# A decoder layer on one Trainium2 core: the key bias added on VectorE, rows normalised on ScalarE

## What is computed

```python
x = x + attention(layernorm(x))        # then cross-attention, then experts
q = xn @ Wq + bq;  k = xn @ Wk + bk;  v = xn @ Wv + bv
Q = elu(q) + 1;    K = elu(k) + 1
KV = einsum('nshd,nshv->nhdv', K, v / L)
Z = 1 / (einsum('nlhd,nhd->nlh', Q, K.sum(axis=1)) + 1e-6)
out = einsum('nlhd,nhdv,nlh->nlhv', Q, KV, Z) * L
```

## Time and profile before

| | |
|---|---|
| median of 3 runs | 1554.05 us (1553.39 to 1558.0) |
| the profiled execution | 1552.01 us, its span 1550.3 us |
| busy over the span: PE, DVE, ACT, POOL | 93%, 40%, 37%, 24% |
| the chain that ended last, by engine | PE 81%, DMA 5%, DVE 4%, issue 4%, POOL 3%, ACT 2% |
| the front | 0 to 293 us |
| TensorE's granted clock, mean | 0.97 of full speed |

### The profile page before, as it was taken

How to read it: one execution, slowest core, us unless ns; L and a number is a source line. 1 busy time by engine, 2 the same in 40 slices (tenths; PEclk the granted TensorE clock), 3 DMA queues, 4 the chain that set the end, 5 groups by cost and what they waited for, 6 DMA issues and landing times.

```text
span 1550.3 us, 20985 instructions
## 1 busy us (share of the span) xinstructions
PE 1447.4 (93%) x7326; PEld 1214.5 (78%) x7327; DVE 623.7 (40%) x1383; ACT 568.7 (37%) x977; POOL 366.3 (24%) x354
## 2 busy tenths in 40 slices
PE   5999999999984499999999899999999999999998
PEld 4867887788772387888888788898789888897886
DVE  5634565467875243411342431215441431215211
ACT  4433433257865233312342531224431422214211
POOL 3201232137665302011112112021112112021011
PEclk9999999999996699999999999999999999999999
DMA  9100221219445426211253432026532342035112
GB/s 198 54 1 28 82 82 55 82 73 219 130 117 173 130 90 163 61 34 20 67 172 54 126 91 41 2 52 184 148 88 54 107 109 41 0 54 149 14 41 27
DMA packets 80537, 132.20 MB, mean 85 GB/s; under 512 B 31940, under 2 KB 32068, under 8 KB 79464
## 3 DMA queue, kind: packets, MB, share of 16 engines
q1 hardware_dynamic: 63816, 97.41, 21.4%
q0 software_dynamic: 16672, 34.16, 11.8%
HBM read 93.64 MB, written 37.91 MB: 85 GB/s over the span
## 4 chain that ended last, share of the span: by engine, by line
PE 81%; DMA 5%; DVE 4%; issue 4%; POOL 3%; ACT 2%; SPq 0%; ACTq 0%; DVEq 0%; POOLq 0%
PE pg L947 16%; PE pg L948 16%; PE pg L949 15%; PE pj L947 8%; PE pj L949 8%; PE pj L948 8%; DMA stage<-w 2%; DMA slot_table<-pack,dest 2%; POOL slot_table L601 2%; PE pt L1301 1%; PE pg L1144 1%; PE pj L1178 1%; DVE w_lo L1364 1%; PE pt L965 1%; DMA out_rows<-ost,etab 1%
## 5 line engine op out<-in xcount | busy, mean ns | idle before, releaser
L947 PE MATMUL pg<-xe_hi,w_hi 128*128 128x512 f32 (+2 forms) x1088 | 393.9, 362 | 22.3 <-DVE w_lo L1364 12.4
L948 PE MATMUL pg<-xe_lo,w_hi 128*128 128x512 f32 (+2 forms) x1088 | 393.0, 361 | 0.0
L949 PE MATMUL pg<-xe_hi,w_lo 128*128 128x512 f32 (+2 forms) x1088 | 392.4, 361 | 0.0
L1755 DVE TENSOR_TENSOR hp<-gl,pg 128x512 f32<-128x512 f32 (+1 forms) x136 | 87.1, 641 | 606.2 <-ACT gl L900 606.2
L678 POOL DMA_INDIRECT out_rows<-ost,etab x62 | 99.8, 1610 | 781.5 <-issue 405.6
L947 PEld LDWEIGHTS pg<-xe_hi,w_hi 128*128 128x128 f32 x1088 | 207.5, 191 | 54.1 <-DVE w_lo L1364 14.4
L900 ACT ACTIVATE gl<-pg 128x512 f32<-128x512 f32 (+1 forms) x136 | 76.1, 560 | 457.2 <-PE pg L949 457.1
L949 PEld LDWEIGHTS pg<-xe_hi,w_lo 128*128 128x128 f32 x1088 | 207.6, 191 | 28.4
L948 PEld LDWEIGHTS pg<-xe_lo,w_hi 128*128 128x128 f32 x1088 | 207.5, 191 | 28.4
L947 PE MATMUL pj<-w_hi,hg_hi 128*128 128x512 f32 x464 | 183.3, 395 | 0.0
L949 PE MATMUL pj<-w_hi,hg_lo 128*128 128x512 f32 x464 | 180.7, 390 | 0.0
(11 more groups left out here) (238 smaller groups left out, 1951.3 us busy)
## 6 DMA issues: line engine op xcount, KB each, us to landing
stage<-w SPq DMA_DIRECT2D x96, 512.0 KB, 4.9
xr<-x SPq DMA_DIRECT2D x8, 1024.0 KB, 8.6
out_rows<-xr SPq DMA_DIRECT2D x8, 1024.0 KB, 7.3
x_rows<-xn SPq DMA_DIRECT2D x8, 1024.0 KB, 6.4
x_in<-x SPq DMA_DIRECT2D x7, 1024.0 KB, 5.2
late_xT<-xT_hi SPq DMA_DIRECT2D x2, 1024.0 KB, 3.9
late_xT<-xT_lo SPq DMA_DIRECT2D x2, 1024.0 KB, 5.9
xT_hi<-late_xT SPq DMA_DIRECT2D x2, 1024.0 KB, 4.7
```

What stands on the lines that cost most here:

```text
L947: nc.tensor.matmul(o, lh, rh, start=start, stop=False)
L948: nc.tensor.matmul(o, lh, rl, start=False, stop=False)
L949: return nc.tensor.matmul(o, ll, rh, start=False, stop=stop)
L1755: v.tensor_tensor(hp[j % 2][:, 0:w], gl[j % 2][:, 0:w], pg[:, 2 + j % 2, 0:w], ALU.mult).then_inc(s_hp, 1)
```

## The change

VectorE has a new step `key_bias`: it adds `bk_all` (the bias on all partitions, loaded by one broadcast transfer) to a key job's bank and writes `kb[j % 2]` in SBUF. ScalarE's exp and relu of key jobs read `kb`. TensorE's 32 bias products go, with `ones_r`, `bk_parts` and their preparation on ScalarE and VectorE, and TensorE's wait for a key bank is now for `s_kb` (VectorE has added) and no longer for `s_feat`. ScalarE's first `wk_hi` waits for `wk_raw` alone.

In each step j of VectorE's loop `key_bias(s, j)` is the first thing, and its feature job is that of j - 1, the `k_lo` that of j - 2. `xn_lo` is made by tiles (`rows_lo`), and the next group's statistics are split in two and two; tiles, statistics and `aggregate` lie between the jobs of steps 0 and 1, the first two statistics ahead of them. Group 0 keeps its four statistics together at the end of step 2.

The rows are normalised on ScalarE (`normalise`, scale and bias from `rstd` and `shift`), behind `k_hi` 1 in step 2, in group 0 behind job 4 and `k_hi` 3 in step 4; VectorE does group 0's own. GpSimd makes `shift` with two more small operations (`neg_mean`, and its product with `rstd`) ahead of the signal.

```diff
...
@@ -192,9 +191,8 @@
     wv_sb = fr("wv_sb", [P, KC, D])
-    ones_r = fr("ones_r", [P, P], F32R)
-    bk_parts = fr("bk_parts", [P, D], F32R)
-    bk_rows = fr("bk_rows", [BR, D])
+    bk_all = fr("bk_all", [P, D])
+    kb = [fr(f"kb{i}", [P, D]) for i in range(2)]
     bv_row = fr("bv_row", [1, D])
...
@@ -372,7 +371,7 @@
         table_t = table[0:TRASH, :].rearrange("(t p) w -> p t w", p=P)
-        XATTN_LOADS, WOUT_LOADS, WK_LOADS, WQ_LOADS, WV_LOADS = 7, 5, 3, 2, 2
+        XATTN_LOADS, WOUT_LOADS, WK_LOADS, WQ_LOADS, WV_LOADS = 7, 5, 1, 2, 2
 
@@ -389,9 +388,8 @@
                 sp.dma_start(x_in[:, i, :], x_g[0][:, i, :]).then_inc(s_x0[i], 16)
-            for dst, src in ((wk_raw[:], wk.rearrange("(k p) n -> p k n", p=P)),
-                             (bk_rows[0:1, :], bk), (bk_rows[BR - 1:BR, :], bk)):
-                sp.dma_start(dst, src).then_inc(s_wk_in, 16)
+            sp.dma_start(wk_raw[:], wk.rearrange("(k p) n -> p k n", p=P)).then_inc(s_wk_in, 16)
+            sp.dma_start(bk_all[:], bk.broadcast_to([P, D])).then_inc(s_bk, 16)
             for dst, src in ((wq_raw[:], wq.rearrange("(k p) n -> p k n", p=P)), (bq_c[:], bq)):
@@ -423,7 +421,7 @@
             sp.wait_ge(s_xnhi, GROUPS)
-            sp.wait_ge(s_xnlo, GROUPS)
+            sp.wait_ge(s_xnlo, GROUPS * TI)
             sp.dma_start(xr[1][:], x_g[1]).then_inc(s_xr[1], 16)
@@ -515,7 +513,13 @@
                 pool.wait_ge(s_stat, s + 1)
-                inverse_std(0).then_inc(s_rstd, 1)
+                if s == 0:
+                    inverse_std(0).then_inc(s_rstd, 1)
+                    return
+                pool.wait_ge(s_xn, s)
+                p.tensor_scalar(neg_mean[0][:], mv[0][:, :, 0], -1.0, None, ALU.mult)
+                step(inverse_std(0))
+                p.tensor_tensor(shift[0][:], neg_mean[0][:], rstd[0][:], ALU.mult).then_inc(s_rstd, 1)
 
@@ -701,13 +705,8 @@
 
-            a.activation(ones_r[:], ones[:], ACT.Copy).then_inc(s_yev, 1)
-            a.activation(bk_parts[:], zrow[:], ACT.Copy).then_inc(s_bk, 1)
             act.wait_ge(s_wk_in, 16 * WK_LOADS)
             a.activation(wk_hi[:], wk_raw[:], ACT.Copy).then_inc(s_whi, 1)
-            act.wait_ge(s_bk, 1)
-            a.activation(bk_parts[0:1, :], bk_rows[0:1, :], ACT.Copy)
-            a.activation(bk_parts[BR - 1:BR, :], bk_rows[BR - 1:BR, :], ACT.Copy).then_inc(s_whi, 1)
 
@@ -718,12 +717,27 @@
             def job(s, j):
-                act.wait_ge(s_proj, FIRST[s] + j + 1)
+                if j < TI:
+                    act.wait_ge(s_kb, s * TI + j + 1)
+                else:
+                    act.wait_ge(s_proj, FIRST[s] + j + 1)
                 if s or j >= 2:
                     act.wait_ge(s_fm, FIRST[s] + j - 1)
-                bias = 0.0 if j < TI else bq_c[:, j - TI:j - TI + 1]
-                a.activation(fe[j % 2][:], pj[j % 2][:], ACT.Exp, bias=bias)
-                a.activation(frl[j % 2][:], pj[j % 2][:], ACT.Relu, bias=bias).then_inc(s_feat, 1)
+                from_, bias = (kb[j % 2], 0.0) if j < TI else (pj[j % 2], bq_c[:, j - TI:j - TI + 1])
+                ins = a.activation(fe[j % 2][:], from_[:], ACT.Exp, bias=bias)
+                if s == 0 and j == 0:
+                    ins.then_inc(s_yev, 1)
+                a.activation(frl[j % 2][:], from_[:], ACT.Relu, bias=bias).then_inc(s_feat, 1)
+
+            def normalise(s):
+
+                act.wait_ge(s_rstd, s + 1)
+                act.wait_ge(s_xnhi, s)
+                act.wait_ge(s_xnlo, s * TI)
+                for i in range(TI):
+                    ins = a.activation(xn[:, i, :], x_in[:, i, :], ACT.Identity, bias=shift[0][:, i:i + 1],
+                                       scale=rstd[0][:, i:i + 1])
+                ins.then_inc(s_xn, 1)
 
@@ -757,6 +771,8 @@
                         khi(s, j - 1)
+                    if s + 1 < GROUPS and j == (TI if s == 0 else 2):
+                        normalise(s + 1)
                     if s == 1 and j == JOBS[s] - 1:
@@ -1029,11 +1045,11 @@
                     if s == 0 and j == 0:
+                        pe.wait_ge(s_whi, 1)
+                        pe.wait_ge(s_wlo, 1)
+                    if s == 0 and j == TI:
                         pe.wait_ge(s_whi, 2)
                         pe.wait_ge(s_wlo, 2)
-                    if s == 0 and j == TI:
-                        pe.wait_ge(s_whi, 3)
-                        pe.wait_ge(s_wlo, 3)
                     if s == 1 and j == TI:
@@ -1044,26 +1060,30 @@
                         value_logits()
-                    if s or j >= 2:
-                        pe.wait_ge(s_feat, FIRST[s] + j - 1)
+
+                    if j >= 2 or s:
+                        b, c = (s, j - 2) if j >= 2 else (s - 1, JOBS[s - 1] + j - 2)
+                        if c < TI:
+                            pe.wait_ge(s_kb, b * TI + c + 1)
+                        else:
+                            pe.wait_ge(s_feat, FIRST[b] + c + 1)
                     o = pj[j % 2][:]
                     if j < TI:
 
                         tk = slice(j * P, (j + 1) * P)
-                        mm(o, ones_r[:], bk_parts[:], start=True, stop=False)
                         for k in range(KC):
                             ins = three(o, x_hi[:, k, tk], x_lo[:, k, tk], wk_hi[:, k, :], wk_lo[:, k, :],
-                                        False, k == KC - 1)
+                                        k == 0, k == KC - 1)
                         ins.then_inc(s_proj, 1)
                     else:
                         q_job(o, slice((j - TI) * P, (j - TI + 1) * P), x_hi, x_lo)
 
             def gram(s, tiles):
 
-                pe.wait_ge(s_xnlo, s + 1)
                 if s % NG == 0 and tiles[0] == 0 and s:
                     pe.wait_ge(s_gev, 2 * (s // NG))
                 for i in tiles:
+                    pe.wait_ge(s_xnlo, s * TI + i + 1)
                     pe.wait_ge(s_klo, s * TI + i + 1)
@@ -1374,13 +1394,22 @@
 
-            def normalise(s):
-
-                dve.wait_ge(s_rstd, s + 1)
+            def normalise_first():
+
+                dve.wait_ge(s_rstd, 1)
                 for i in range(TI):
                     ins = v.tensor_scalar(xn[:, i, :], x_in[:, i, :], mv[0][:, i, 0:1], rstd[0][:, i:i + 1],
                                           ALU.subtract, ALU.mult)
                 ins.then_inc(s_xn, 1)
+
+            def key_bias(s, j):
+
+                dve.wait_ge(s_proj, FIRST[s] + j + 1)
+                if s or j >= 2:
+
+                    b, c = (s, j - 2) if j >= 2 else (s - 1, TI + j - 2)
+                    dve.wait_ge(s_feat, FIRST[b] + c + 1)
+                v.tensor_tensor(kb[j % 2][:], pj[j % 2][:], bk_all[:], ALU.add).then_inc(s_kb, 1)
 
@@ -1474,6 +1503,7 @@
                 dve.wait_ge(s_xin, 16 * s)
+                dve.wait_ge(s_rstd, s)
                 link(stats(x_in, 0, range(TI)))
@@ -1482,25 +1512,42 @@
             aggregate(0, s_stat)
-            normalise(0)
+            normalise_first()
             dve.wait_ge(s_whi, 1)
             low(wk_lo[:], wk_raw[:], wk_hi[:]).then_inc(s_wlo, 1)
-            dve.wait_ge(s_whi, 2)
-            low(bk_parts[BR - 1:BR, :], bk_rows[BR - 1:BR, :], bk_parts[BR - 1:BR, :]).then_inc(s_wlo, 1)
+            dve.wait_ge(s_bk, 16)
+
+            def rows_lo(s, tiles):
+
+                dve.wait_ge(s_xnhi, s + 1)
+                for i in tiles:
+                    low(xn_lo[:, i, :], xn[:, i, :], xn_hi[:, i, :]).then_inc(s_xnlo, 1)
+
+            def keys_lo(s, i):
+
+                dve.wait_ge(s_khi, s * TI + i + 1)
+                dve.wait_ge(s_fm, FIRST[s] + i + 1)
+                low(k_lo[:, i, :], kf[i % 2][:], k_hi[:, i, :]).then_inc(s_klo, 1)
+
+
 
             for s in range(GROUPS):
                 turned_lo(s)
                 if s == NG:
                     gram_out(0)
-                dve.wait_ge(s_xnhi, s + 1)
-                low(xn_lo[:], xn[:], xn_hi[:]).then_inc(s_xnlo, 1)
+                ahead = 1 <= s < GROUPS - 1
                 if s == 0:
-                    dve.wait_ge(s_whi, 3)
+                    rows_lo(0, range(TI))
+                    dve.wait_ge(s_whi, 2)
                     low(wq_lo[:], wq_raw[:], wq_hi[:]).then_inc(s_wlo, 1)
                     v.tensor_scalar(bq_neg[:], bq_c[:], -1.0, None, ALU.mult)
-                if s >= 1 and s + 1 < GROUPS:
-                    next_stats(s + 1)
-                for j in range(max(JOBS[s], TI + 1)):
+                if ahead:
+                    dve.wait_ge(s_xin, 16 * (s + 1))
+                    dve.wait_ge(s_rstd, s + 1)
+                    stats(x_in, 0, range(2))
+                if s:
+                    rows_lo(s, range(1))
+                for j in range(JOBS[s] + 2):
                     if s == 1 and j == TI:
@@ -1509,16 +1556,22 @@
                         value_logits_out()
-                    if j < JOBS[s]:
-                        job(s, j)
-                    if 1 <= j <= TI:
```

(23 more changed lines are left out.)

## The result

The changed kernel takes 1546.1 us (median of 14 runs, 1543.31 to 1551.85) against 1553.72 beside it (14 runs): a ratio of 0.9946 by all the runs, 95% interval 0.9926 to 0.9967, 0.54% faster (the two medians alone give 0.9951). Its profiled execution took 1546.13 us (span 1544.3), before 1552.01 (span 1550.3).

A forecast was written before the change was run, and what follows sets the result against it. TensorE was taken to bound the attention front (busy 272.0 us of 0 to 293). The terms -7.3 - 1.1 - 3.6 - 0.6 + 2.2 = -10.4 us took the median from 1554.05 to 1543.7 us; range 1537.0 to 1550.5.

The forecast's parts named there:

- Step 1: Attention front, TensorE's queue: 32 bias products removed at 0.227 us each, nothing hiding them; -7.3 us.
- Step 4: Groups 5 and 6: ScalarE normalising ends the xn wait, a new xT_lo wait replaces most; -0.6 us in all.
- step 3: Group 2: TensorE's wait for vpT falls from 2.7 to 0.8 us, without a slower clock; -3.6 us.
- Step 2: Start of the front: VectorE's bias low part goes, ScalarE waits for wk_raw alone; -1.1 us.
- The 1.78: Upper bound in us for VectorE's key bias addition beside GpSimd's k_sum; the forecast took 0.69.
- Step 5: Groups 1 to 3: ScalarE's job 4 waits behind normalising; cost 0, with nothing in hand in group 3.
- Step 6: Group 0: new TensorE wait, job 5 being queued behind ScalarE's normalising; +2.2 us, of which 1.85 at one stroke.
- It moves as a block: Behind the front: the same program, released the same way, shifts as a whole without its stages changing length.
- (a): Rival: the clock falls in group 0, the forecast plus 1.7 us, 1545.4 us; chance 0.12.
- (b): Rival: no new wait and all the old ones gone, -16.4 us, 1537.7 us; chance 0.17.
- (c): Rival: VectorE bounds groups 2, 5 and 6, additions beside k_sum taking 1.78 us; 1550.3 us; chance 0.13.
- (d): Rival: GpSimd's factors come late and ScalarE's queue stands; slower, 1563.2 us from 3 us late; chance 0.06.

The follow-up runs named there:

- the three mends: The changed kernel plus early table load, group 0 normalised behind job 5, xT_lo ahead of the last k_lo in groups 5 and 6: 1540.55 us, 0.9914.

## Why the prediction was right, step by step

The forecast of 1543.7 us was 2.4 us under the 1546.1 measured: it had the medians 10.4 us apart, and beside each other they were 7.6 apart. The sign and the mechanism hold, several terms were off, and part of the front's 9.35 us is luck. `wk_raw` happened to land 0.79 us earlier, and the slow first products took 0.73 us less (the first fourteen 4.94 us, 5.67 before), which differs from run to run. Without both the front gained 7.8 us, 2.5 less than forecast: 1.6 are missing at the start, 0.7 in groups 5 and 6, 0.4 in group 7 and 0.2 in group 3, and group 2 gave 0.3 more.

**Step 1, the bias products.** As a sum it holds (0.95 us in group 1 and 0.91 in group 4, where nothing else changed the length), but not as a term of its own. "They sit in TensorE's busy queue, so nothing hides them" is wrong wherever a wait follows: taken out alone they brought a ratio of 0.999, nothing that can be told from no change. Step 4's and step 3's waits had to go as well, and ScalarE's normalising alone brings nothing sure either (0.9986). Both of these with `vpT` ahead of job 3 bring the groups to 264.79 us, within 1.4 of the whole change's 263.39. In group 7 the change earned 0.47 of 0.91: its first gram product starts 0.54 us behind the product ahead of it (0.23 elsewhere), at 271.55, when VectorE has ended `k_lo` 0 (270.72 to 271.40), behind two `xn_lo` that took 2.39 us beside a `k_sum` and the key bias 2. In group 3 it earned 0.70.

**Step 2, the start.** Predicted -1.1, measured -0.33: the table load was missed. From the landing to the first product it is 19.58 - 10.47 = 9.11 us before and 9.57 after: 0.84 less to do and 1.30 more, 0.46 lost. Only the earlier landing (0.79) made it a gain, and that is chance: the last load that ScalarE waits for landed at 9.06 to 10.68 in the five kernels with `bk_rows` and at 9.22 to 10.83 in the nine without. So the 0.4 put down for `bk_rows` shows in no run. The broadcast of `bk` cost nothing that shows.

**Step 3, group 2.** Predicted 41.65 - 0.91 - 3.6 = 37.1, measured 36.88. The wait left is 0.4 (predicted 0.8), and the clock stayed up. The key bias took its 0.69 even beside `k_sum` (seven of the 32 ran beside one for 0.54 us or more): GpSimd's order of time, then VectorE's, in group 6:

```profile
244.83 3.18 POOL L562 TENSOR_TENSOR k_sum<-k_sum,kf 128x512 f32<-128x512 f32 x2
```

```profile
246.25 0.69 DVE L1412 TENSOR_TENSOR kb<-pj,bk_all 128x512 f32<-128x512 f32 x1 [0.83 <-PE pj L965]
246.85 1.70 DVE L1431 SCALAR_TENSOR_TENSOR kf<-fe,frl 128x512 f32<-128x512 f32 x1
248.48 0.68 DVE L1384 TENSOR_TENSOR k_lo<-kf,k_hi 128x512 fp32r<-128x512 f32 x1
```

The 1.78 did come, but on `kf` (1.70 us, two inputs from SBUF), and `k_lo` 1 behind it took 0.68: the same length of queue by another instruction. The Trainium skill's rule ("SBUF — State Buffer", "Who interferes with whom"), by which a VectorE instruction with two SBUF inputs contends with GpSimd's reads and one with at most one, outside its two-port modes, doesn't, agrees with both rows. The prediction left out the two-port modes, and without them its sentence doesn't hold here: VectorE's normalising reads one tile from SBUF, and took 1.51 us beside `k_sum` and 0.54 by itself. Whether it ran in such a mode isn't shown. The layout by hand was right in its times, and it had `vpT` ahead of job 3; but the text blamed the statistics and the normalising. The runs show that the statistics' place does nothing here, that the normalising has to leave VectorE, and that the copy's place then decides.

**Step 4, groups 5 and 6.** Predicted 24.9, measured 25.2, with the wait for `xT_lo` named (1.0 predicted, 1.25 measured). The factors were ready at 9.7 (`shift` at 244.53 to 244.87, the group's start at 235.16), predicted 9.9. `kf` 3 took 1.03 instead of 0.69, as long as the difference.

**Step 5.** Groups 1 to 3 should have cost nothing; group 3 fell 0.2 us short of its four products, group 1 not at all.

**Step 6, group 0.** The wait is where it was forecast, at 42.05, with no fall of the clock. It is listed with 1.45 us, but a product is listed with 0.39 us where the next can start after 0.23: the distance over the wait is 1.84 us instead of 0.23, and the next one is 0.1 too long, so it cost 1.7 us (forecast 1.85). The two small terms came too: products behind jobs' starts at 34.70, 35.04 and 37.90 stand 0.30 to 0.34 apart, 0.3 us in all (forecast 0.1 and 0.2). The group's length was forecast at 37.87 - 0.91 + 2.2 = 39.16 and was 38.37. The difference is the slow start: how many first products run at half pace differs from run to run (7 in after, 11 before, 13 in two experiments), and with the 0.73 us that this profile had less, the group comes to 39.10.

**"It moves as a block."** The medians agree with this step, and no single pair of profiles can show it. The part behind the front, the same program in all fourteen profiles, lasted from 1256.5 to 1272.2 us (the span less the end of the front), a spread wider than the whole gain. Nearly all of the spread lies between the first product of routing (`pj<-hot,tri`) and the first turning for the experts (`pt<-ident,xg`), 185.9 to 199.2 us; from the first `pj<-w_hi,hg_hi` on, the experts took 974.3 to 975.1. TensorE in the routing stage, kernel after:

```profile
446.00:450.50 4.50, 3.61 (x16) 3.39 (x17) 3.86 (x17) 3.27 (x7) 3.43 (x3) 0.50 0.01 0
450.50:461.00 10.50, 10.50 (x37) 7.69 (x37) 7.16 (x36) 6.58 (x15) 6.22 (x8) 0.56 0.90 199
```

The grant was 0.50 and 0.56 there; in the kernel before it was 0.89 at the same distance from the front's end (455.35 to 470.35). But over 120 us from 400 the two are at 0.73 and 0.75, so the clock is one thing that differs and not shown to be the cause of the 3.4 us. The medians follow the front: the three mends shorten it by 4.2 us and the median by 4.1, the products alone by nothing that shows in either, and the whole change by 7.8 at an equal start and 7.6. Their intervals are 3 to 6 us to either side, so this agrees with the step and doesn't prove it. A single profile's total can't carry a gain of 10 us; the lengths of groups 1 to 7, equal to 0.1 us between two profiles of the changed kernel, can.

**The rivals.** (a) didn't come: no fall in group 0. (b) didn't: old waits were replaced, not removed. (c) is dead by 32 additions of 657 to 693 ns. (d) didn't: it needed factors past 10.7, and they came at 9.7. Its "a wait past 2 us brings 1.7 us of half clock" isn't borne out as a rule: two waits of 3.2 us brought none. The range's lower end, 1537.0, stands 0.7 under (b)'s time and not at it, which changes nothing.

## What to carry to other kernels

Work taken from the engine that bounds a stage turns into waiting if its suppliers come no earlier, and a slower clock can eat the rest; look first at what the next wait is for. In a queue written by hand, ask of each instruction that the bounding engine waits for whether something it doesn't need stands ahead of it: here moving one copy of 0.85 us gave 3.3 to 3.9 us, once ScalarE normalised. The room on an engine must be counted with what runs beside it: a tile normalised on VectorE costs 0.54 us or 1.51. When an engine's first small instructions are removed as useless, see what loaded under them.

## What the runs showed of the hardware

- The clock fell behind waits of TensorE of 2.0 (the kernel with ScalarE's normalising alone), 2.1, 2.2, 2.3, 2.7, 2.9 and 3.6 us, and not behind waits of 1.3, 1.45 and, unexpectedly, 3.2 us. So the length of the wait alone doesn't decide it; what does stays open.
- Where it fell in group 2, the half pace lasted 3.0 to 3.4 us, which costs some 1.6, and 4.7 us behind the wait of 2.0, the shortest. The wait of 2.1 us with `vpT` behind made group 2 3.3 us longer, though the wait itself grew only 1.7.
- At the start the first 7 to 13 products run 0.43 us apart while the grant is listed as 1.00. What sets that pace isn't shown.
- VectorE's normalising of one tile took 0.53 to 0.54 us, and 1.5 beside one of GpSimd's `k_sum`; of four tiles 2.88 us with one such (the kernel before) and 3.86 with two. ScalarE's took 2.91 to 2.93 in every group of the kernel after, beside `k_sum` too.
- VectorE's additions of PSUM and SBUF took 0.69 us beside `k_sum` and without it; its operations with two SBUF inputs 0.68 without it and 1.70 (`kf`) or 1.78 (`k_lo`) beside it.
